# A windowed-attention kernel on one core: the fourth scores of image 0 move to other banks, v's projection and the first bias move ahead of them, and image 1's middle parts are placed behind the first Exp

## The chip, the cores and the metric

The program runs on one core of a Trainium2 chip. The core has five engines with instruction streams of their own: TensorE (PE, matrix products), VectorE (DVE), ScalarE (ACT), GpSimd (POOL) and SyncE (SP, which here only issues transfers), and 16 DMA engines shared by all queues. The engines wait for each other on counting semaphores. The metric is the device time of one execution in microseconds (us); lower is better.

## The reference

One block of a shifted-window transformer on 8 images of 16 x 128 tokens with 32 channels; windows of 4 x 32 tokens (16 windows for each image, N = 128 tokens each), 4 heads of 8 channels:

```python
y = _layernorm(x, g1, b1)
y = jnp.roll(y, (-SH, -SW), axis=(1, 2))
xw = windows(y)                                    # (B * NWIN, N, DIM)
qkv = (xw @ qkv_w + qkv_b)
q, k, v = (qkv[0] * SCALE, qkv[1], qkv[2])
attn = jnp.einsum('bhid,bhjd->bhij', q, k) + bias + mask
attn = jax.nn.softmax(attn, axis=-1)
o = jnp.einsum('bhij,bhjd->bhid', attn, v) @ proj_w + proj_b
x = x + unroll(o)
z = _layernorm(x, g2, b2)
z = gelu(z @ fc1_w + fc1_b) @ fc2_w + fc2_b
return x + z
```

The lines `windows` and `unroll` stand for the reshapes of the reference; `bias` is a relative-position table and `mask` hides windows' foreign regions.

## The kernel before

**Units of work.** The 128 windows are taken in 64 pairs (PAIRS), 8 pairs an image. For a pair j the kernel computes the scores twice: scores 1 (`bias_s1`, `scores_s1`, query rows on the partitions), of which DVE takes the row maximum (`row_max`, L524, into `negm`), and scores 2 (`bias_s2`, `scores_s2`, key rows on the partitions), into which the maximum has already been fed as extra rows of q, and of which ACT takes the exponential (`exponential`, L735, into `prob`). `weighted_values` (L945) multiplies the exponentials with v. For every two pairs (a group k) PE transposes the maxima (`transpose_max`, L863), ACT rounds them to bf16 (`high_max`, L730, `m_hi`), DVE takes what is left (`middle_max`, L530, `m_mid`), and SP sends both into `q_rows` (`send_max`, L262); the first scores 2 of the group wait for these transfers (semaphores d_m0 and d_m1).

**Each image's preparation.** PE transposes the normalized image (`transpose_first`, L839), ACT copies it (`copy_yT`, L708), PE projects q and k (`project_qk`, L845) and v (`project_v`, L851). q and k are then split into three bf16 parts: the high part by ACT (`high_part`, L713), the remainder by DVE (`remainder`, L515), the middle part by ACT (`middle_part`, L719), the low part by POOL (`low_part`, L394), each for two halves. SP stores a part in DRAM (`scatter`, L250) and twelve gathers (`gather`, L212, each 16 x 8 x 512 bf16, 128 KB) bring the parts back as rows. The scores 1 of an image's first pair wait for all twelve (`scores_s1`: semaphore d_qk); for image 1 that is pair 8. Image 0 takes a shorter way for its first pairs and is not gathered whole.

**PSUM.** Two banks each: `ps1`, `ps2`, `pq` (halves Q0 and Q1); one bank each: `pav`, `pch`. Scores 1 of pairs 1 and 3 are put in ps2 by `first_home`, all others in ps1. Scores 2 are always in ps2, and the projection of v of image 0 and the transposes of image 2 both use Q0.

**What sets the order.** No scheduler: every engine has a hand-written loop over p from -4 (LEAD = 4) to 63, and what stands in iteration p runs in the order of the `if` lines. Scores 1 run four pairs ahead: iteration p issues scores 1 of pair p + 4 and scores 2 of pair p. Iterations -4 to -1 are the opening. A bank is free for the next bias only when its reader is done: `bias_s1(j)` waits for j maxima, `bias_s2(j)` for j exponentials.

The lines that matter in the opening are `pe.wait_ge(max_done, LEAD)` before the first `bias_s2` (L906), the wait for `mmid_done` before `project_qk` in iteration 1 (L1071), and ACT's iteration -1 (L810 to L816), whose `middle_part(1, 0)` and `middle_part(1, 1)` stand ahead of everything of iteration 0.

## Time and profile before

| what | us |
|---|---|
| median of 3 runs | 231.94 |
| the runs | 230.03, 231.94, 233.01 |
| the profiled execution | 230.33 |
| its span (first to last instruction) | 228.5 |
| PE busy in the span | 208.5 |
| DVE, ACT, POOL busy | 165.0, 148.6, 128.2 |

The profiled execution took 230.33 us, of which 228.5 us are the span and 1.8 us lie around it. Its times are counted from the span's start. A row of the timeline has the start, the duration, engine, source line, operation, output and inputs, and in brackets the engine's idle time before it and what ended it. Rows of the same kind that overlap are merged (x8), and the two passes of an fp32 matmul count as two. SPq and ACTq are the issuing of transfers by those engines. A row of a stretch has from:to, its length, the busy us of PE, PE's weight loads, DVE, ACT and POOL (instructions in brackets), PE's granted clock (1.00 is full speed), the mean busy share of the 16 DMA engines and what they moved in GB/s.

### The profile page before, as it was taken

The page shows a single profiled execution, that of the slowest core. Times are in us where ns is not written, and L with a number is a line of the kernel's source. Part 1 is how long each engine was busy: PE and PEld are TensorE (multiplying, and loading weights), DVE is VectorE, ACT ScalarE, POOL GpSimd, SP SyncE. Part 2 cuts the span into 40 slices and gives each one's busy share as a digit, 9 for nine tenths or more (in the row PEclk, how much of TensorE's full clock was granted, in tenths as well). Part 3 has the DMA queues.
Part 4 walks back from the last instruction along what each step waited for, and adds up shares of the span by engine and source line. Part 5 has one row for each costly group of instructions (what it writes and reads, how often), then busy time and mean ns, then how long its engine had stood idle before and what let it go on. Part 6 is the DMA issues. An engine that isn't in the chain of part 4 may idle for free.

```text
span 228.5 us, 8108 instructions
## 1 busy us (share of the span) xinstructions
PE 208.5 (91%) x3342; PEld 118.3 (52%) x3342; DVE 165.0 (72%) x253; ACT 148.6 (65%) x217; POOL 128.2 (56%) x116
## 2 busy tenths in 40 slices
PE   0779966899999999999999999999999999979884
PEld 0734523556565556655655566566556555443221
DVE  3896756666877777878787877786766757866874
ACT  7475167656676677677757775867555555577883
POOL 8765669272447956794778397632742092160740
PEclk9997999999999999999999999999999999999999
DMA  6826346654524532452255045405520000000233
GB/s 196 244 74 178 108 131 195 177 170 150 165 72 148 164 102 96 144 163 80 95 166 163 11 136 166 122 10 164 179 83 4 6 6 4 1 3 0 105 127 138
DMA packets 24284, 25.41 MB, mean 111 GB/s; under 512 B 3556, under 2 KB 21732, under 8 KB 24164
## 3 DMA queue, kind: packets, MB, share of 16 engines
q1 hardware_dynamic: 23496, 24.16, 34.0%
q10 hardware_dynamic: 752, 0.74, 1.2%
q8 instruction: 26, 0.43, 0.8%
q14 instruction: 10, 0.08, 0.1%
HBM read 16.24 MB, written 8.39 MB: 108 GB/s over the span
## 4 chain that ended last, share of the span: by engine, by line
issue 39%; POOL 36%; PE 10%; ACT 6%; DVE 3%; DMA 2%; SPq 1%; POOLq 1%; ACTq 0%; DVEq 0%
POOL rstd L376 17%; POOL X L406 4%; POOL parts L394 4%; POOL yn L386 3%; POOL X L411 3%; POOL xc L368 3%; PE ps L962 3%; DMA slots<-parts 2%; ACT q_rows L740 1%; POOL mean L356 1%; ACT k_rows L740 1%; POOL var L362 1%; PE pq L962 1%; PE pav L992 1%; ACT k_rows L745 1%
## 5 line engine op out<-in xcount | busy, mean ns | idle before, releaser
L524 DVE TENSOR_REDUCE negm<-ps 128x8 f32<-128x1024 f32 x64 | 78.2, 1223 | 32.7 <-PE ps L898 32.5
L735 ACT ACTIVATE prob<-ps 128x1024 f32<-128x1024 f32 x64 | 65.5, 1023 | 39.7 <-PE ps L925 39.6
L376 POOL TENSOR_TENSOR rstd<-var,neghalf 128x16 f32<-128x16 f32 x16 | 47.4, 2962 | 17.3 <-DVE var L489 16.4
L912 PE MATMUL ps<-rel_j,id_b 96*32 96x512 bf16 x512 | 39.5, 381 | 3.1 <-ACT prob L735 2.9
L945 PE MATMUL pav<-prob,va 128*32 128x128 f32 x1024 | 41.1, 279 | 0.0
L945 PEld LDWEIGHTS pav<-prob,va 128*32 128x32 f32 x1024 | 24.1, 109 | 12.5 <-issue 5.0
L876 PE MATMUL ps<-rel_i,ident_b 64*64 64x512 bf16 x256 | 26.7, 407 | 0.2 <-DVE negm L524 0.2
L925 PE MATMUL ps<-q_rows,k_rows 64*128 64x128 bf16 x512 | 25.4, 219 | 0.4 <-DMA q_rows<-m_mid 0.4
L898 PE MATMUL ps<-k_rows,q_rows 64*128 64x128 bf16 x512 | 25.2, 219 | 0.0
L394 POOL TENSOR_TENSOR parts<-rest,parts 128x512 bf16<-128x512 f32 x15 | 17.3, 1158 | 13.6 <-ACT parts L719 13.6
L925 PEld LDWEIGHTS ps<-q_rows,k_rows 64*128 64x128 bf16 x512 | 14.4, 94 | 15.5 <-issue 14.6
L730 ACT ACTIVATE m_hi<-pq 16x128 bf16<-16x128 f32 x32 | 8.5, 265 | 16.6 <-PE pq L863 16.5
L356 POOL TENSOR_SCALAR mean<-ssum 128x16 f32<-128x16 f32 x11 | 2.8, 257 | 29.0 <-DVE ssum L471 28.6
L898 PEld LDWEIGHTS ps<-k_rows,q_rows 64*128 64x128 bf16 x512 | 17.0, 95 | 1.3 <-issue 1.3
L876 PEld LDWEIGHTS ps<-rel_i,ident_b 64*64 64x64 bf16 x256 | 7.2, 103 | 18.2 <-DVE negm L524 7.9
L912 PEld LDWEIGHTS ps<-rel_j,id_b 96*32 96x32 bf16 x512 | 11.8, 96 | 9.0 <-ACT prob L735 8.5
L530 DVE TENSOR_TENSOR m_mid<-pq,m_hi 16x128 bf16<-16x128 f32 x32 | 8.6, 270 | 8.7 <-ACT m_hi L730 7.4
L386 POOL TENSOR_TENSOR yn<-xc,rstd 128x512 f32<-128x512 f32 x13 | 13.9, 1071 | 1.0
L368 POOL TENSOR_TENSOR xc<-X,mean 128x512 f32<-128x512 f32 x12 | 12.6, 1048 | 1.7 <-DVE yn L504 0.8
L362 POOL TENSOR_SCALAR var<-vsum 128x16 f32<-128x16 f32 x11 | 2.2, 203 | 19.9 <-DVE vsum L483 19.6
L471 DVE TENSOR_REDUCE ssum<-X 128x16 f32<-128x512 f32 x16 | 10.9, 681 | 2.7 <-DMA X<-x_tok 2.5
L515 DVE SCALAR_TENSOR_TENSOR rest<-pq,qk_bias,parts 128x512 f32<-128x512 f32 x12 | 8.9, 745 | 4.3 <-ACT parts L713 4.3
(134 smaller groups left out, 333.8 us busy)
## 6 DMA issues: line engine op xcount, KB each, us to landing
slots<-parts SPq DMA_DIRECT2D x21, 256.0 KB, 2.4
q_rows<-slots SPq DMA_DIRECT2D x42, 128.0 KB
k_rows<-slots SPq DMA_DIRECT2D x40, 128.0 KB
X<-x_tok SPq DMA_DIRECT2D x8, 256.0 KB, 4.0
y_tok<-res SPq DMA_DIRECT2D x7, 256.0 KB, 2.0
q_rows<-m_hi SPq DMA_DIRECT2D x32, 4.0 KB
q_rows<-m_mid SPq DMA_DIRECT2D x32, 4.0 KB
bias_parts<-rel_parts SPq DMA_DIRECT2D x3, 128.0 KB
```

The lines of the kernel that those rows point to most:

```text
L368: pool.tensor_tensor(per_window(xc[:, i, :]), per_window(img(n)), mean[:, i, :].unsqueeze(2).to_broadcast([128, WPI, C]), ALU.subtract).th ...
L376: pool.tensor_tensor(rstd[:, i, :], var[:, i, :], neghalf[:], ALU.pow).then_inc(rstd_done[i], 1)
L386: pool.tensor_tensor(per_window(yn[:, i, :]), per_window(xc[:, i, :]), rstd[:, i, :].unsqueeze(2).to_broadcast([128, WPI, C]), ALU.mult).t ...
L394: pool.tensor_tensor(parts[:, n % 2, LOW, u, :], rest[:, u, :], parts[:, n % 2, MID, u, :], ALU.subtract).then_inc(lo_done, 1)
L471: dve.tensor_reduce(ssum[:, i, :], per_window(img(n)), AX.X, ALU.add).then_inc(sum_done[i], 1)
L524: dve.tensor_reduce(dst, first_home(j)[:].rearrange("p (a u n) -> p a u n", u=2, n=TOK), AX.X, ALU.max, negate=True).then_inc(max_done, 1)
L735: act.activation(prob[:, j % NPROB, :], ps2[:], ACT.Exp).then_inc(exp_done, 1)
L876: pe.matmul(home[64 * c:64 * (c + 1), 512 * e:512 * (e + 1)], ident_b[64 * e:64 * (e + 1), 64 * e:64 * (e + 1)], rel_i[64 * e:64 * (e + 1) ...
L898: mm = pe.matmul(home[:, 512 * e + at:512 * e + at + TOK], q_rows[64 * e:64 * e + 64, b % NBUF, rows], k_rows[64 * e:64 * e + 64, b % NBUF ...
L912: pe.matmul(ps2[32 * c:32 * (c + 1), 512 * e:512 * (e + 1)], id3_b[0:96, :], rel_j[0:96, c, e].unsqueeze(2).to_broadcast([96, 2, 2, TOK]), ...
L925: mm = pe.matmul(ps2[:, 512 * e + at:512 * e + at + TOK], k_rows[64 * e:64 * e + 64, b % NBUF, rows], q_rows[64 * e:64 * e + 64, b % NBUF, ...
L945: mm = pe.matmul(pav[32 * h:32 * (h + 1), 128 * (j % 4):128 * (j % 4 + 1)], va[:, b % 2, at:at + 32], prob[:, j % NPROB, src:src + 128], s ...
```

## The change

Three edits, all in the opening; every instruction of before is still there.

1. `first_home(3)` is ps1, not ps2. So ps2 is free for `bias_s2(0)` as soon as two maxima are done (the wait for LEAD becomes one for 2), and `bias_s1(3)` must now wait for 3 maxima and not 2.
2. On PE, iteration -1 begins with `project_v(0)` and `bias_s2(0)`, ahead of scores 1 of pair 3. In iteration 0 the transposes of image 2 and `scores_s2(0)` come first, and `transpose_max(1)` and `bias_s1(4)` follow.
3. On ACT, image 1's two middle parts move from iteration -1 to behind the Exp of pair 0. What needs them moves too: on SP the scatter of the middle part goes from iteration -2 to 0, the two low gathers from iteration 0 to 2, behind the maxima of group 2; on ACT the two gathers of the middle part of k go from iteration 0 to 2, behind the Exp of pair 2. On DVE, `middle_max(1)` goes ahead of image 3's sums, and `row_max(5)` ahead of image 2's first remainder.

```diff
--- before.py
+++ after.py
@@ -118,7 +118,7 @@
         FC1 = (ps1, pq, ps2)
 
         def first_home(j):
-            return ps2 if j in (1, 3) else ps1
+            return ps2 if j == 1 else ps1
 
         def mlp_home(m, lo):
             return (pav, pch)[m % 2] if m < B - 1 else (Q1 if lo else Q0)
@@ -287,12 +287,13 @@
                     gather(sp, b + 1, LOW, 1)
                 if p == -2:
                     scatter(1, HIGH)
-                    scatter(1, MID)
                     gather(sp, 1, HIGH, 0)
                 if p == 0:
+                    scatter(1, MID)
+                    gather(sp, 1, HIGH, 1)
                     scatter(1, LOW)
-                    gather(sp, 1, HIGH, 1)
                     gather(sp, 1, MID, 0)
+                if p == 2:
                     gather(sp, 1, LOW, 0)
                     gather(sp, 1, LOW, 1)
                 if p == 3:
@@ -635,11 +636,15 @@
                 n = b + 2
                 if p % 4 == 0 and 0 <= (p - 8) // 4 < OCTETS:
                     add_attention((p - 8) // 4)
+                if p == 0:
+                    middle_max(1)
                 if s == 0 and 3 <= b + 3 < B:
                     dve.wait_ge(d_x[b + 3], 16)
                     sums(first_norm(b + 3), b + 3)
                 if p % 4 == 2 and 0 <= (p - 6) // 4 < OCTETS:
                     normalize((p - 6) // 4)
+                if p == 1:
+                    row_max(p + LEAD)
                 if p >= 0 and n < B and s in (1, 3):
                     remainder(n, s // 2, (Q1, Q0)[s // 2])
                 if s == 6 and 0 <= b - 2 < B - 2:
@@ -653,9 +658,9 @@
                     square_sums(second_norm(b - 1))
                 if s == 7 and b == B - 1:
                     scale(second_norm(b - 1))
-                if p % 2 == 0 and 0 <= (p + 2) // 2 < GROUPS:
+                if p and p % 2 == 0 and (p + 2) // 2 < GROUPS:
                     middle_max((p + 2) // 2)
-                if 0 <= p < PAIRS - LEAD:
+                if 0 <= p < PAIRS - LEAD and p != 1:
                     row_max(p + LEAD)
                 if s == 4 and b == B - 1:
                     dve.wait_ge(x2_done, 2 * b)
@@ -804,6 +809,9 @@
                 if 0 <= p < PAIRS:
                     exponential(p)
                 if p == 0:
+                    middle_part(1, 0)
+                    middle_part(1, 1)
+                if p == 2:
                     gather(act, 1, MID, 1)
                 if p >= 0 and n < B and s in (1, 3):
                     middle_part(n, s // 2)
@@ -812,8 +820,6 @@
                     values(0)
                     high_part(1, 0, pav[:])
                     high_part(1, 1, pch[:])
-                    middle_part(1, 0)
-                    middle_part(1, 1)
                 if s == 3 and 3 <= b + 3 < B:
                     square(first_norm(b + 3))
                 if s == 5 and 0 <= b - 1 < B - 2:
@@ -867,8 +873,8 @@
                 if j < 2:
                     pe.wait_ge(q_first, 1)
                     pe.wait_ge(k_first, 1)
-                elif j < LEAD:
-                    after(pe, max_done, j - 1)
+                elif j == 2:
+                    pe.wait_ge(max_done, 1)
                 else:
                     pe.wait_ge(max_done, j)
                 for c in range(2):
@@ -903,7 +909,7 @@
 
             def bias_s2(j):
                 if j == 0:
-                    pe.wait_ge(max_done, LEAD)
+                    pe.wait_ge(max_done, 2)
                     pe.wait_ge(d_relj, 16)
                     pe.wait_ge(ident_ready, 2)
                 after(pe, exp_done, j)
@@ -1077,17 +1083,22 @@
                         pe.wait_ge(rest_done, 2 * n + 2)
                     project_v(b + 1)
 
+                if p == -1:
+                    project_v(0)
+                    bias_s2(0)
                 if p < 0:
                     bias_s1(p + LEAD)
                     scores_s1(p + LEAD)
                 if p == -3:
                     pe.wait_ge(q_first, 2)
                     keep_busy(3, Q0[:, 0:128])
-                if p == -1:
-                    project_v(0)
+                if p == 0:
+                    pe.wait_ge(va_done, n - 1)
+                    transpose_first(n, Q0)
+                    scores_s2(p)
                 if 0 <= p - AV_LAG < PAIRS:
                     weighted_values(p - AV_LAG)
-                if 0 <= p < PAIRS:
+                if 0 < p < PAIRS:
                     bias_s2(p)
                 if p % 2 == 0 and 0 <= (p + 2) // 2 < GROUPS:
                     transpose_max((p + 2) // 2)
@@ -1097,11 +1108,7 @@
                     project_qk(1, (pch[:], pav[:]))
                 if 0 <= p < PAIRS - LEAD:
                     bias_s1(p + LEAD)
-                if p == 0:
-                    pe.wait_ge(va_done, n - 1)
-                    transpose_first(n, Q0)
-
-                if 0 <= p < PAIRS:
+                if 0 < p < PAIRS:
                     scores_s2(p)
                 if 0 <= p < PAIRS - LEAD:
                     scores_s1(p + LEAD)
```

On PE, from the first group's transposed maxima (L863) to image 2's projection (the last row of each); `ps1<-rel_i` is a bias of scores 1, `ps1<-k_rows,q_rows` scores 1, `ps2<-rel_j` a bias of scores 2, `ps2<-q_rows,k_rows` scores 2, and `pq<-wv_s,yT` v's projection. Before:

```order
L845 MATMUL pav<-yT,wqk_s 128x512
L876 MATMUL ps2<-rel_i,ident_b 64x512 [waits max_done]
L898 MATMUL ps2<-k_rows,q_rows 128x128 x8
L851 MATMUL pq<-wv_s,yT 128x128 x4
L912 MATMUL ps2<-rel_j,id3_b 32x512 [waits ident_ready,d_relj,max_done]
L863 MATMUL pq<-par,negm 16x128 [waits yT_done,mmid_done,max_done]
L876 MATMUL ps1<-rel_i,ident_b 64x512 [waits max_done]
L839 MATMUL pq<-par,yn 128x128 [waits yn_done0,va_done]
L925 MATMUL ps2<-q_rows,k_rows 128x128 [waits d_m0]
L898 MATMUL ps1<-k_rows,q_rows 128x128 [waits d_aux0,d_first]
L845 MATMUL pq<-yT,wqk_s 128x512 [waits yT_done,mmid_done]
```

and after the change:

```order
L851 MATMUL pav<-yT,wqk_s 128x512
L857 MATMUL pq<-wv_s,yT 128x128 x4
L918 MATMUL ps2<-rel_j,id3_b 32x512 [waits ident_ready,d_relj,max_done]
L882 MATMUL ps1<-rel_i,ident_b 64x512 [waits max_done]
L904 MATMUL ps1<-k_rows,q_rows 128x128 x8
L845 MATMUL pq<-par,yn 128x128 [waits yn_done0,va_done]
L931 MATMUL ps2<-q_rows,k_rows 128x128 [waits d_m0]
L869 MATMUL pq<-par,negm 16x128 [waits yT_done,mmid_done,max_done]
L882 MATMUL ps1<-rel_i,ident_b 64x512 [waits max_done]
L904 MATMUL ps1<-k_rows,q_rows 128x128 [waits d_aux0,d_first]
L851 MATMUL pq<-yT,wqk_s 128x512 [waits yT_done,mmid_done]
```

The scores 1 of pair 3 (now in ps1) stand behind v's projection and the first bias of scores 2; the second transposed maxima and the bias for pair 4 stand behind the scores 2 of pair 0.

On ACT, from behind image 1's high parts on, with the Exps (`prob<-ps2`), the parts of images 1 and 2 and the k_rows gathers. Before:

```order
L719 ACTIVATE parts<-rest 128x512 [waits rest_done] x2
L708 ACTIVATE yT<-pq 128x512 [waits vp_done,yTp_done0]
L730 ACTIVATE m_hi<-pq 16x128 [waits mT_done]
L735 ACTIVATE prob<-ps2 128x1024 [waits s2_done]
L212 DMA k_rows<-slots 16x8x512 [waits zero_k1,d_scr_mid]
L212 DMA k_rows<-slots 16x8x512
L713 ACTIVATE parts<-pq,qk_bias 128x512 [waits d_scr_hi,qk_done]
L735 ACTIVATE prob<-ps2 128x1024 [waits s2_done]
L719 ACTIVATE parts<-rest 128x512 [waits d_scr_mid,rest_done]
L713 ACTIVATE parts<-pq,qk_bias 128x512 [waits d_scr_hi,qk_done]
L730 ACTIVATE m_hi<-pq 16x128 [waits d_m0,mT_done]
L735 ACTIVATE prob<-ps2 128x1024 [waits s2_done] x2
```

and after the change:

```order
L713 ACTIVATE yT<-pq 128x512 [waits vp_done,yTp_done0]
L735 ACTIVATE m_hi<-pq 16x128 [waits mT_done]
L740 ACTIVATE prob<-ps2 128x1024 [waits s2_done]
L724 ACTIVATE parts<-rest 128x512 [waits rest_done] x2
L718 ACTIVATE parts<-pq,qk_bias 128x512 [waits d_scr_hi,qk_done]
L740 ACTIVATE prob<-ps2 128x1024 [waits s2_done]
L724 ACTIVATE parts<-rest 128x512 [waits d_scr_mid,rest_done]
L718 ACTIVATE parts<-pq,qk_bias 128x512 [waits d_scr_hi,qk_done]
L735 ACTIVATE m_hi<-pq 16x128 [waits d_m0,mT_done]
L740 ACTIVATE prob<-ps2 128x1024 [waits s2_done]
L212 DMA k_rows<-slots 16x8x512 [waits zero_k1,d_scr_mid]
L212 DMA k_rows<-slots 16x8x512
```

The two middle parts (x2, `parts<-rest`) moved behind the first Exp, and the two gathers from behind the first Exp to behind the third.

On SP, from group 1's m_mid to image 1's last low gather; `slots<-parts` are scatters, `q_rows<-m_hi` and `q_rows<-m_mid` the maxima. A piece of the difference:

```order
 L262 DMA q_rows<-m_mid 2x8x128 [waits mmid_done]
-L250 DMA slots<-parts 128x2x512 [waits lo_done]
+L250 DMA slots<-parts 128x2x512 [waits mid_done]
 L212 DMA k_rows<-slots 16x8x512 [waits zero_k1,d_scr_hi]
 L212 DMA k_rows<-slots 16x8x512 x2
+L250 DMA slots<-parts 128x2x512 [waits lo_done]
 L212 DMA q_rows<-slots 16x8x512 [waits zero_q1,d_scr_mid]
 L212 DMA q_rows<-slots 16x8x512
+L262 DMA q_rows<-m_hi 2x8x128 [waits mhi_done]
+L262 DMA q_rows<-m_mid 2x8x128 [waits mmid_done]
 L212 DMA q_rows<-slots 16x8x512 [waits zero_q1,d_scr_lo]
 L212 DMA k_rows<-slots 16x8x512 [waits zero_k1,d_scr_lo]
```

The middle scatter, and behind it the low scatter, come later, and the maxima of group 2 go out before the two low gathers.

## Rows read from the trace of the kernel before

**Rows 1.** The page's first rows: the span, and each engine's busy time.

```profile
span 228.5 us, 8108 instructions
...
PE 208.5 (91%) x3342; PEld 118.3 (52%) x3342; DVE 165.0 (72%) x253; ACT 148.6 (65%) x217; POOL 128.2 (56%) x116
```

**Rows 2.** Stretches from:to, length, each engine's busy us, granted clock, DMA share, GB/s.

```profile
28.00:32.00 4.00, 2.27 (x33) 1.15 (x33) 2.16 (x4) 3.66 (x8) 2.19 (x3) 1.00 0.20 67
...
36.00:44.00 8.00, 6.15 (x118) 2.97 (x119) 5.01 (x7) 5.07 (x10) 5.38 (x7) 1.00 0.57 173
...
44.00:66.00 22.00, 22.00 (x397) 13.29 (x393) 16.13 (x23) 14.82 (x24) 8.14 (x8) 1.00 0.47 144
```

**Rows 3.** Timeline of PE, 25 to 33 us: start, duration, line, operation, [idle before].

```profile
25.90 0.41 PE L876 MATMUL ps<-rel_i,ident_b 64*64 64x512 bf16 x4
...
26.57 1.16 PE L851 MATMUL pq<-wv_s,yT 128*128 128x128 f32 x8
...
27.97 0.61 PE L912 MATMUL ps<-rel_j,id_b 96*32 96x512 bf16 x8 [0.23 <-DVE negm L524]
...
29.06 0.66 PE L839 MATMUL pq<-par,yn 128*128 128x128 f32 x4
...
32.18 1.13 PE L845 MATMUL pq<-yT,wqk_s 64*128 64x512 f32 x4 [1.91 <-DVE m_mid L530]
```

**Rows 4.** Timeline of ACT, 28 to 39 us.

```profile
28.89 0.69 ACT L713 ACTIVATE parts<-pch,qk_bias 128x512 bf16<-128x512 f32 x1
...
29.89 1.29 ACT L719 ACTIVATE parts<-rest 128x512 bf16<-128x512 f32 x2 [0.31 <-DVE rest L515]
...
31.56 0.25 ACT L730 ACTIVATE m_hi<-pq 16x128 bf16<-16x128 f32 x1
...
31.72 1.00 ACT L735 ACTIVATE prob<-ps 128x1024 f32<-128x1024 f32 x1
...
33.36 1.22 ACTq L212 DMA_DIRECT2D k_rows<-slots  x2
...
34.68 0.69 ACT L713 ACTIVATE parts<-pq,qk_bias 128x512 bf16<-128x512 f32 x1 [1.97 <-issue]
...
35.27 1.01 ACT L735 ACTIVATE prob<-ps 128x1024 f32<-128x1024 f32 x1
...
36.25 0.63 ACT L719 ACTIVATE parts<-rest 128x512 bf16<-128x512 f32 x1
...
38.40 1.02 ACT L735 ACTIVATE prob<-ps 128x1024 f32<-128x1024 f32 x1 [0.41 <-PE ps L925]
```

**Rows 5.** Timeline of DVE, 25 to 37 us: maxima, m_mid, remainder.

```profile
25.49 2.42 DVE L524 TENSOR_REDUCE negm<-ps 128x8 f32<-128x1024 f32 x2
...
31.84 0.28 DVE L530 TENSOR_TENSOR m_mid<-pq,m_hi 16x128 bf16<-16x128 f32 x1 [0.74 <-ACT m_hi L730]
...
35.47 0.75 DVE L515 SCALAR_TENSOR_TENSOR rest<-pq,qk_bias,parts 128x512 f32<-128x512 f32 x1 [2.22 <-ACT parts L713]
```

**Rows 6.** Timeline of POOL: image 2 normalized.

```profile
27.74 1.05 POOL L386 TENSOR_TENSOR yn<-xc,rstd 128x512 f32<-128x512 f32 x1
```

**Rows 7.** Timeline of PE: scores 2 of pair 4, scores 1 of pair 8.

```profile
43.45 0.40 PE L925 MATMUL ps<-q_rows,k_rows 64*128 64x128 bf16 x8 [0.41 <-DMA q_rows<-m_mid]
...
43.69 0.39 PE L898 MATMUL ps<-k_rows,q_rows 64*128 64x128 bf16 x8
```

**Rows 8.** SP's queue: three k gathers, the last low gather, group 2's m_mid.

```profile
35.52 2.96 SPq L212 DMA_DIRECT2D k_rows<-slots  x3
...
40.51 0.59 SPq L212 DMA_DIRECT2D k_rows<-slots  x1
...
41.74 0.53 SPq L262 DMA_DIRECT2D q_rows<-m_mid  x1
```

**Rows 9.** Stretch in which SP's gathers run, columns as in rows 2.

```profile
40.00:41.00 1.00, 1.00 (x28) 0.65 (x28) 0.57 (x1) 0.20 (x1) 0.45 (x1) 1.00 0.71 223
```

**Rows 10.** Line L212, 25 to 50 us: issue duration ns min/median/max.

```profile
L212 SPq DMA_DIRECT2D k_rows<-slots x4: 590/598/1681, 35.5 to 40.5; - x4
```

## Prediction

> **What bounds the kernel now.** I read the stretches first. From 44 us on PE is busy for all 22.00 us of the first full image's 22.00 us at granted clock 1.00, and the page gives PE 91% of the span [rows 1, 2]. The chain of waits ends over POOL, but POOL idles there; the PE rows decide. So a microsecond won after 44 us would have to come out of PE's work, and this change adds and removes no instruction. Before 44 us it is different: between 28 and 32 us PE works 2.27 of 4.00 us, between 36 and 44 us 6.15 of 8.00 us [rows 2]. What the change can win is idle time of PE in the opening, and what it wins shows as the start of PE's full stretch moving left. I take as its mark the scores 1 of pair 8, the first pair of image 1, now at 43.69 us [rows 7]; everything behind it slides with it.
>
> The largest hole is the 1.91 us before image 2's projection at 32.18 us [rows 3]. It is ended by DVE's m_mid (31.84 to 32.12 us) [rows 5], which waits for ACT's m_hi at 31.56 us, and ACT came to that late since two middle parts of image 1 (29.89 us, 1.29 us long) and a copy stood ahead of it [rows 4]. The second hole is before Exp 1: ACT issues two gathers at 33.36 us (1.22 us), so its high part starts only at 34.68 us, 1.97 us after the last work, and Exp 1 at 35.27 us [rows 4].
>
> **The change, walked through.** All times are worked out from the rows; small starts of 0.05 to 0.1 us are included.
>
> PE. Bias and scores 1 of pair 3 took 25.90 to 26.57 us, 0.67 us. With them behind, v's projection starts at 25.90 us and not 26.57 us, and ends at about 27.0 us; ACT's high parts, which follow it, end at 28.9 us and not at 29.58 us. The first bias of scores 2 (0.61 us) takes PE to 27.6 us; it needs two maxima only, so its old wait of 0.23 us is gone. Scores 1 of pair 3 end at 28.3 us. Their maximum (half of 2.42 us, now done at 27.91 us) runs from 28.3 to 29.5 us: 1.6 us later than now. This is the price of the edit. POOL's normalized image 2 is there at 28.79 us, so the transposes run from 28.85 to 29.5 us, against 29.06 to 29.72 us now, and scores 2 of pair 0 end at 29.9 us. The second transposed maxima follow and need the late maximum (29.5 us): there is 0.4 us to spare, so the price is covered [rows 3 to 6].
>
> ACT and DVE. Without the middle parts ahead, m_hi of group 1 ends at 30.45 us (31.81 now) and Exp 0 starts at 30.35 us (31.72 now). But m_mid does not come as early: on DVE two remainders of 0.75 us stand ahead of it, behind the late maximum, from 29.5 to 31.0 us, so m_mid ends at 31.25 us and the projection starts at 31.3 us, 0.9 us earlier than now [rows 3 to 5].
>
> Pair 1: from 31.3 us the projection (1.13), a bias of scores 2 (0.61), a bias and the scores (0.34 and 0.40) give Exp 1 at 33.85 us with 0.1 us for the fourth maximum, since image 3's sums now stand ahead of it; ACT has by then done Exp 0, the middle parts (to 32.65 us) and the high part. Exp 1 is 1.4 us earlier. Pair 2: the maximum of pair 5 now stands ahead of image 2's remainder, which therefore ends at about 36.0 us, hardly before the 36.22 us of now; ACT's copy of it (36.25 us now) comes at 36.1 us, and high part and m_hi follow. Exp 2 starts at 37.4 us instead of 38.40 us: 1.0 us is left [rows 4, 5]. From there to pair 4 the order is the old one. Scores 2 of pair 4 start at 43.45 us after 0.41 us of waiting for m_mid's transfer; that transfer goes out ahead of the low gathers now, so the wait falls away as well. The mark stands, as far as the engines go, at 43.69 - 1.0 - 0.41 = 42.3 us: **1.4 us is the upper bound of the gain** [rows 4, 7].
>
> SP and the transfers. The mark waits for all twelve gathers of image 1. Now the last is issued at 40.51 us [rows 8]. Between the maxima of group 1 and that gather SP now issues 1 scatter, 3 + 2 gathers and the two low ones; after, it issues also the middle scatter and the two transfers of group 2's maxima: 0.4 + 0.55 + 0.53 = 1.5 us more. Its start is 0.6 us earlier with the high parts. One of the three k gathers took 1.68 us to issue against a median of 0.60 [rows 8, 10]; it followed ACT's two gathers. If the long one is gone, the last gather goes out at 40.51 + 1.5 - 0.6 - 1.1 = 40.3 us; if it returns behind ACT's gathers, which now stand behind Exp 2 at 38.4 to 39.7 us, at 41.4 us. To land it needs no more than the 2.9 us from 40.51 us to 43.45 us, at which the transfer issued behind it had landed [rows 7, 8], and I take 2.4 us. So the rows of image 1 are there between 42.7 and 43.8 us, middle 43.2 us, which is later than 42.3 us. **I expect a gain of 43.7 - 43.2 = 0.5 us**, between 0 and 1.0 us.
>
> POOL gets the middle parts 1.5 us later and its low parts with them, but SP reaches the low scatter only at about 36.5 us, and POOL had idle time before; this costs nothing unless the low scatter were to stand ahead of the k gathers.
>
> A word on bytes: between 40 and 41 us the queues moved 223 GB/s at a share of 0.71 [rows 9]. ACT's two gathers (256 KB) left their place before SP's rush and stand in it now; at that rate they need 1.2 us of the DMA engines beside the last four gathers. The Trainium skill, "DMA: Bandwidth & Descriptors", section "Issuing engines are not separate DMA queues", says that transfers of all issuing engines run on the same 16 DMA engines and interleave, so that a second queue saves only issue time. Taken at its word it adds those 1.2 us to the landing, 44.4 us at the middle, and the kernel is slower by 0.7 us; the trace, with its share of 0.71, leaves room for part of it.
>
> **The sum.** 228.5 - 0.5 = 228.0 us of span, 229.8 us for an execution like the profiled one (230.33). The median of the runs shown, 231.94 us, is 1.6 us above that execution, so I place the median after at 231.94 - 0.5 = 231.4 us.
>
> **The rivals.**
> - *The rows of image 1 come in time*: SP's long issue is gone and the gathers land before 42.3 us. For it: between 36 and 44 us the DMA share is only 0.57 [rows 2]. Against it: the low gathers wait for the low scatter, and seven transfers are issued serially. Gain 1.4 us: 230.5 us. Chance 0.2.
> - *Nothing*: the rows land about as late as the mark of now, and each 0.1 us won is idle time before pair 8. 231.9 us. Chance 0.15.
> - *Slower*: the rows land later than 43.7 us; this is the point from which it decides, and PE has then nothing else to do, as v's projection and the weighted values of pair 3 are queued behind. With the long issue (41.4 us), 2.9 us to land and ACT's bytes (1.2 us) it is 45.5 us, a loss of 1.8 us: 233.7 us; half of that at the middle, 232.8 us. Chance 0.2.
> - *The maxima become the limit*: DVE's remainders ahead of m_mid take longer than thought, and the projection stays near 32.18 us. Then Exp 1 still gains from ACT's free time; 231.7 us. It lies inside the forecast.
>
> **The numbers.** The forecast (gain 0.2 to 1.0 us) has 0.45, and the three rivals 0.2, 0.15 and 0.2. The likeliest gives 231.4 us. The runs of before spread from 230.03 to 233.01 us, more than any case here moves, so the range takes the profiled execution with the larger gain (230.33 - 1.3 = 229.0) to the median with the slower case (233.0). Two per cent is 4.6 us, about what a measurement of this kernel can tell from no change. The holes of the opening that could be won are near that in sum (1.73 us of 28 to 32, 1.85 us of 36 to 44 [rows 2]) and cannot all close: faster 0.02. To be slower by 4.6 us the rows of image 1 would have to land at 48 us: 0.03. Within 2%: 0.95.
>
> **What would show it.** In the changed kernel's timeline: v's projection at 25.9 us; transposed maxima of group 1 about 30 us and m_mid ended at 31.3 us; image 2's projection at 31.3 us with a hole below 1 us; Exp 0, 1 and 2 at 30.4, 33.9 and 37.4 us. No wait for m_mid's transfer before scores 2 of pair 4, and instead a wait for a gather before scores 1 of pair 8, which start at 43.2 us. PE full from there, and the span shorter by the same amount. Wrong would be: a mark later than 43.7 us (the slower rival), a mark at 42.3 us without a wait (the first rival), or a shift at the mark that is not found again at the end.

## The result, and the profile of the changed kernel

The changed kernel is slower. Its executions have a median of 234.3 us (4, from 233.04 to 236.09); beside them the kernel before has 231.31 us (4, from 230.03 to 233.01). The ratio is 1.018, with a 95% interval of 1.011 to 1.025: some 3 us more, on the other side of the forecast and above its range. Four later executions (label a1) gave 1.018 again.

The profiled execution took 233.04 us. First rows of its page (columns of the groups: busy us, mean ns of one, idle just before them and what ended it):

```profile
span 231.2 us, 8108 instructions
...
PE 209.2 (90%) x3342; PEld 118.9 (51%) x3342; DVE 164.9 (71%) x253; ACT 148.6 (64%) x217; POOL 128.3 (55%) x116
...
L904 PE MATMUL ps<-k_rows,q_rows 64*128 64x128 bf16 x512 | 24.8, 216 | 2.5 <-DMA k_rows<-slots 2.5
...
L931 PE MATMUL ps<-q_rows,k_rows 64*128 64x128 bf16 x512 | 25.4, 219 | 0.6 <-DMA q_rows<-m_mid 0.6
```

2.7 us were added to the span [rows 1] and only 0.7 us of it to PE's busy time. The wait before scores 1 (L904) is new: 2.5 us, once, for the gathered rows of k. The stretches, columns as in [rows 2]:

```profile
28.00:32.00 4.00, 3.09 (x33) 1.49 (x37) 3.85 (x6) 2.63 (x6) 0.89 (x2) 1.00 0.24 77
36.00:44.00 8.00, 4.88 (x101) 2.43 (x97) 3.57 (x5) 4.89 (x9) 6.62 (x7) 1.00 0.62 189
44.00:50.00 6.00, 5.17 (x63) 3.84 (x64) 2.00 (x3) 1.60 (x3) 2.68 (x2) 0.72 0.52 173
50.00:66.00 16.00, 16.00 (x292) 9.16 (x290) 11.71 (x17) 10.07 (x17) 5.21 (x6) 1.00 0.46 137
```

From 28 to 32 us PE works 0.8 us more than in [rows 2]. That alone does not show the hole filled by the edit: an execution of the kernel before with its clock at 1.00 in the opening (label b2) has 3.13 us there. From 24 to 32 us together it is 6.73 us after against 5.86 us in b2, and this 0.9 us is the filled idle time. From 36 to 44 us PE works 1.3 us less than in [rows 2]. From 44 to 50 us it falls short of full, and at a mean granted clock of 0.72, so that part of the stretch ran at the lower of the two levels. From 50 us on all is as before. PE's timeline (start, duration, line, operation, [idle before]; L857 is v's projection, L845 the transposes of image 2, L851 its projection, L931 scores 2, L904 scores 1):

```profile
25.20 1.16 PE L857 MATMUL pq<-wv_s,yT 128*128 128x128 f32 x8
...
28.91 0.63 PE L845 MATMUL pq<-par,yn 128*128 128x128 f32 x4 [1.24 <-POOL yn L387]
...
30.75 1.13 PE L851 MATMUL pq<-yT,wqk_s 64*128 64x512 f32 x4
...
41.89 0.40 PE L931 MATMUL ps<-q_rows,k_rows 64*128 64x128 bf16 x8 [0.62 <-DMA q_rows<-m_mid]
44.83 0.40 PE L904 MATMUL ps<-k_rows,q_rows 64*128 64x128 bf16 x8 [2.54 <-DMA k_rows<-slots]
45.16 2.08 PE L857 MATMUL pq<-wv_s,yT 128*128 128x128 f32 x8
...
49.15 0.40 PE L931 MATMUL ps<-q_rows,k_rows 64*128 64x128 bf16 x8
```

The mark, scores 1 of pair 8, stands at 44.83 us instead of 43.69 us [rows 7]. Behind it v's projection takes 2.08 us and not 1.16 us, and scores 2 of the next pair start 4.32 us after the mark, against 2.75 to 2.77 us where the clock stays at 1.00 (experiments e1 and e4): 1.6 us for the clock. 1.1 + 1.6 = 2.7 us, the whole difference between the two profiled executions. Against b2 it is 1.4 + 1.6 = 3.0 us, and the spans differ by 2.9 us. ACT's and DVE's timelines (L740 is Exp, L724 the middle parts; on DVE L531 is m_mid):

```profile
30.29 1.00 ACT L740 ACTIVATE prob<-ps 128x1024 f32<-128x1024 f32 x1
31.19 1.13 ACT L724 ACTIVATE parts<-rest 128x512 bf16<-128x512 f32 x2
...
33.25 1.02 ACT L740 ACTIVATE prob<-ps 128x1024 f32<-128x1024 f32 x1 [0.36 <-PE ps L931]
...
36.66 1.00 ACT L740 ACTIVATE prob<-ps 128x1024 f32<-128x1024 f32 x1
```

```profile
30.41 0.28 DVE L531 TENSOR_TENSOR m_mid<-pq,m_hi 16x128 bf16<-16x128 f32 x1 [0.15 <-ACT m_hi L735]
```

Exp 0, 1 and 2 are earlier than in [rows 4] by 1.4, 2.0 and 1.7 us, m_mid than in [rows 5] by 1.4 us. Part of that is this execution's clock (below); in any case the engines came earlier, and the end of the opening did not. SP's queue says why:

```profile
33.92 2.95 SPq L212 DMA_DIRECT2D k_rows<-slots  x3
36.92 0.59 SPq L250 DMA_DIRECT2D slots<-parts  x1
...
39.51 0.52 SPq L262 DMA_DIRECT2D q_rows<-m_mid  x1
41.22 0.56 SPq L212 DMA_DIRECT2D q_rows<-slots  x1
41.88 0.56 SPq L212 DMA_DIRECT2D k_rows<-slots  x1
```

SP sends the low scatter (L250) at 36.92 us, finishes with m_mid's transfer of group 2 at 40.03 us, and has then nothing to do but the two low gathers. It issues them at 41.22 and 41.88 us, since they wait for that scatter to land: 4.3 us after its issue. The last of them is in 2.95 us after its issue. In [rows 8] the last gather had gone out at 40.51 us, *ahead* of m_mid. The DMA engines in the 40 slices of 0.25 us from 36 to 46 us (first line tenths busy, second GB/s):

```profile
DMA  0367384789799999897400001047447954854976
GB/s 16 70 209 234 111 270 152 201 266 258 258 361 356 357 352 299 258 316 255 130 29 25 20 0 33 0 131 242 152 115 221 340 209 164 262 197 115 287 238 254
```

Between 38 and 40.5 us they move up to 361 GB/s; from 41.0 to 42.5 us almost nothing, while PE waits. From 41.0 us on the wait is not for bandwidth but for an order: landing of the scatter, issue, landing. Whether the scatter itself landed late because of the traffic over it (mean DMA share 0.80 from 36.9 to 41.2 us), these rows don't separate.

### The profile page after: what moved, and what is told of

The parts are those of the page before. It is cut to its first block, busy times and chain, and to the rows that moved or that the text cites. A ratio compares the mean times of both kernels' runs of the same rounds, so it can differ in the third digit from the quotient of the medians.

```text
span 231.2 us, 8108 instructions
## 1 busy us (share of the span) xinstructions
PE 209.2 (90%) x3342; PEld 118.9 (51%) x3342; DVE 164.9 (71%) x253; ACT 148.6 (64%) x217; POOL 128.3 (55%) x116
## 4 chain that ended last, share of the span: by engine, by line
issue 43%; POOL 41%; PE 6%; ACT 4%; DVE 3%; DMA 2%; POOLq 1%; DVEq 0%
POOL rstd L377 18%; POOL parts L395 5%; POOL X L407 4%; POOL yn L387 4%; POOL xc L369 3%; POOL X L412 3%; PE ps L968 2%; DMA X<-x_tok 2%; ACT q_rows L745 1%; POOL mean L357 1%; POOL var L363 1%; ACT k_rows L745 1%; PE pq L968 1%; PE pav L998 1%; POOL va L335 1%
## 5 line engine op out<-in xcount | busy, mean ns | idle before, releaser
L740 ACT ACTIVATE prob<-ps 128x1024 f32<-128x1024 f32 x64 | 65.5, 1024 | 40.0 <-PE ps L931 39.9
L951 PE MATMUL pav<-prob,va 128*32 128x128 f32 x1024 | 41.6, 281 | 0.0
L951 PEld LDWEIGHTS pav<-prob,va 128*32 128x32 f32 x1024 | 24.3, 110 | 12.7 <-issue 5.3
L904 PE MATMUL ps<-k_rows,q_rows 64*128 64x128 bf16 x512 | 24.8, 216 | 2.5 <-DMA k_rows<-slots 2.5
L882 PE MATMUL ps<-rel_i,ident_b 64*64 64x512 bf16 x256 | 26.2, 400 | 0.3 <-DVE negm L525 0.2
L931 PE MATMUL ps<-q_rows,k_rows 64*128 64x128 bf16 x512 | 25.4, 219 | 0.6 <-DMA q_rows<-m_mid 0.6
L931 PEld LDWEIGHTS ps<-q_rows,k_rows 64*128 64x128 bf16 x512 | 14.4, 94 | 15.7 <-issue 14.6
L904 PEld LDWEIGHTS ps<-k_rows,q_rows 64*128 64x128 bf16 x512 | 16.7, 94 | 3.8 <-issue 3.8
L531 DVE TENSOR_TENSOR m_mid<-pq,m_hi 16x128 bf16<-16x128 f32 x32 | 8.6, 270 | 9.1 <-ACT m_hi L735 7.8
L1049 PE MATMUL pch<-par,oT 128*128 128x128 f32 x64 | 10.5, 287 | 1.2 <-DVE oT L627 1.2
```

What stands on the lines that cost most here:

```text
L740: act.activation(prob[:, j % NPROB, :], ps2[:], ACT.Exp).then_inc(exp_done, 1)
L882: pe.matmul(home[64 * c:64 * (c + 1), 512 * e:512 * (e + 1)], ident_b[64 * e:64 * (e + 1), 64 * e:64 * (e + 1)], rel_i[64 * e:64 * (e + 1) ...
L904: mm = pe.matmul(home[:, 512 * e + at:512 * e + at + TOK], q_rows[64 * e:64 * e + 64, b % NBUF, rows], k_rows[64 * e:64 * e + 64, b % NBUF ...
L931: mm = pe.matmul(ps2[:, 512 * e + at:512 * e + at + TOK], k_rows[64 * e:64 * e + 64, b % NBUF, rows], q_rows[64 * e:64 * e + 64, b % NBUF, ...
L951: mm = pe.matmul(pav[32 * h:32 * (h + 1), 128 * (j % 4):128 * (j % 4 + 1)], va[:, b % 2, at:at + 32], prob[:, j % NPROB, src:src + 128], s ...
```

## A table to compare like with like

Executions of one kernel differ in when the granted clock is at 0.5, and the opening shifts with it: with 20 to 24 us at 1.00, 0.57 or 0.50, scores 1 of pair 2 stand at 23.3 to 23.6, 24.3 to 24.5 or 25.0 to 26.7 us. I therefore compare the mark only within a class. The last class is the roughest: e2 starts from 25.0 us and b1 from 26.1 us, so that e2's figure is rather too small, and b1 and e10 had a second fall ahead of the mark (0.60 from 36 to 40 us, 0.57 from 40 to 44 us) that e6, for one, did not have. "Before" has an execution in each (labels b2, the profiled one, b1).

| 20–24 us at | kernel: mark, us | against before |
|---|---|---|
| 1.00 | before 43.44; after 44.83 and 44.57; e1 43.73; e4 44.26; e5 43.84; e7b 42.30 | after +1.4, +1.1; e1 +0.3; e4 +0.8; e5 +0.4; e7b −1.1 |
| 0.57 | before 43.69; e3 44.30; e7 43.06 | e3 +0.6; e7 −0.6 |
| 0.50 | before 45.08; e2 46.44; e6 45.11; e8 47.56; e8b 47.05; e10 46.41; e11 48.00 | e2 +1.4; e6 0.0; e8 +2.5; e8b +2.0; e10 +1.3; e11 +2.9 |

The mark carries through to the end. Span less mark is 184.8 to 184.9 us in the ten profiled executions whose clock stays at 1.00 behind the mark (before, b1, b2, e1, e4 to e7b, e10), and 186.3 to 186.5 us in the five where it falls there for a few us (after, a1, e2, e3, e8b); in e8 and e11, where it falls for longer, 187.6 and 187.1 us. So a fall behind the mark costs 1.5 to 1.6 us, and all else that these kernels differ in is decided at the mark.

By the same token one execution is a thin base. Spans of all executions with a mean granted clock of 0.998 or more:

| kernel | span, us |
|---|---|
| before | 227.0 to 229.2, median 227.4 (30); b2 is one of 228.3 |
| e1 | 228.6, 228.8 |
| e2 | 228.8 |
| e3 | 228.5, 228.6 |
| e4 | 229.1 to 230.6, median 230.1 (5) |
| e5 | 228.4 to 228.7 (4) |
| e6 | 227.0 to 227.7 (3) |
| e7 and e7b | 226.2 to 227.1 (8) |
| e8 | 227.4 |
| after and a1, e8b, e10, e11 | none |

b2's mark of 43.44 us is thus late for a "before" at full clock: 227.4 less 184.85 us puts a typical one at about 42.5 us (an estimate), and the losses in the first row of the table are rather too small, by up to 0.9 us.

Against b2, the execution of before at 1.00, the engines' gain has the places that the prediction had, at a third to three quarters of the size: image 2's projection 31.18 → 30.75 us, Exp 1 34.26 → 33.25 us, Exp 2 37.39 → 36.66 us, scores 2 of pair 4 43.21 → 41.89 us. And b2 says one thing more:

```profile
31.18 1.13 PE L845 MATMUL pq<-yT,wqk_s 64*128 64x512 f32 x4 [0.64 <-DVE m_mid L530]
...
43.21 0.40 PE L925 MATMUL ps<-q_rows,k_rows 64*128 64x128 bf16 x8 [1.17 <-DMA q_rows<-m_mid]
43.44 0.39 PE L898 MATMUL ps<-k_rows,q_rows 64*128 64x128 bf16 x8
```

```profile
34.49 3.65 SPq L212 DMA_DIRECT2D k_rows<-slots  x3
...
40.35 0.55 SPq L212 DMA_DIRECT2D k_rows<-slots  x1
...
41.54 0.53 SPq L262 DMA_DIRECT2D q_rows<-m_mid  x1
```

The projection is 1.0 us earlier than in the profiled execution [rows 3], the mark only 0.25 us [rows 7]. The rest is a wait of 1.17 us for the transfer of m_mid, which SP issued at 41.54 us behind its gathers; three k gathers alone held the queue for 3.65 us. With the clock up, the opening of *before* was already bound by SP's queue, in this execution at least. The 0.41 us of [rows 7] was the tip of that wait, and the profiled execution hid it since its engines came late.

## Experiments

Ratios are against the kernel before in runs side by side; the expectations speak of the mark and of distances from scores 1 of pair 2 to it. Where only a part of an edit is shown, dots stand for the rest.

**e1: the edits on PE alone** (fourth scores in ps1 instead of ps2, v's projection and first bias up), all of the middle parts as before.

```
-            return ps2 if j in (1, 3) else ps1
+            return ps2 if j == 1 else ps1
...
+                if p == -1:
+                    project_v(0)
+                    bias_s2(0)
...
```

> Only edits 1 and 2 (bank of pair 3's scores, v's projection and the first bias moved up); ACT, DVE and SP as before. Theory L (the loss comes from image 1's rows, which edit 3 makes late, and from the clock that falls while PE waits for them): no wait for a gather before the scores 1 of pair 8, which start at 43.0 to 43.7 us; ratio to before 0.99 to 1.002. Theory P (PE's new order costs the time, since the maximum of pair 3 is 1.6 us later): the mark is later than 44 us and the ratio above 1.01.

231.83 us (10), ratio 1.0075 (1.002 to 1.013), between the ranges of the two theories: no wait for a gather, but not without a loss either. The late fourth maximum is not free. DVE, ACT and PE:

```profile
27.65 1.23 DVE L524 TENSOR_REDUCE negm<-ps 128x8 f32<-128x1024 f32 x1 [0.84 <-PE ps L898]
28.79 0.74 DVE L515 SCALAR_TENSOR_TENSOR rest<-pav,qk_bias,parts 128x512 f32<-128x512 f32 x1
```

```profile
29.57 1.29 ACT L719 ACTIVATE parts<-rest 128x512 bf16<-128x512 f32 x2 [1.61 <-DVE rest L515]
```

```profile
43.49 0.40 PE L925 MATMUL ps<-q_rows,k_rows 64*128 64x128 bf16 x8 [0.80 <-DMA q_rows<-m_mid]
43.73 0.39 PE L898 MATMUL ps<-k_rows,q_rows 64*128 64x128 bf16 x8
```

The maximum of pair 3 starts at 27.65 us and both remainders behind it; ACT waits 1.61 us for them and has the middle parts 0.7 us later than before at the same clock (29.57 against 28.89 us). With them go the middle scatter and all that SP sends behind it, and the 0.80 us for m_mid at 43.49 us are what is left of that. (In the changed kernel itself this does not bind: the remainders are done at 30.26 us, and the middle parts start at 31.19 us, behind Exp 0.)

**e2: the middle parts and the new order of the transfers alone.**

```
                 if p == -2:
                     scatter(1, HIGH)
-                    scatter(1, MID)
...
                 if p == 0:
-                    scatter(1, LOW)
+                    scatter(1, MID)
                     gather(sp, 1, HIGH, 1)
+                    scatter(1, LOW)
                     gather(sp, 1, MID, 0)
+                if p == 2:
                     gather(sp, 1, LOW, 0)
...
```

> Only edit 3 (image 1's middle parts behind the first Exp, with the moved scatter and gathers); PE's order and banks as before. Theory L: the low gathers are issued at 41 to 42 us, the scores 1 of pair 8 wait 1 to 3 us for them and start at 44.5 to 45.5 us, the clock falls behind that wait, ratio 1.01 to 1.02. Theory P: no such wait, ratio below 1.005.

234.73 us (4), against 230.26 us of before; there is no ratio. By the table +1.4 us at the mark, and the clock fell behind it. At a mean clock of 0.978 its three executions have spans of 232.9 to 233.7 us, where before has a median of 231.2 us and e1, at 0.977 and 0.978, 230.9 to 231.7 us: there this edit loses some 2 us and e1 hardly anything. With the clock at 1.00 its one execution (228.8 us) is no longer than e1's. So most of the loss is in this edit where the clock falls; its share at full clock is not shown.

```profile
44.88 0.40 PE L931 MATMUL ps<-q_rows,k_rows 64*128 64x128 bf16 x8 [1.85 <-DMA q_rows<-m_mid]
46.44 0.40 PE L904 MATMUL ps<-k_rows,q_rows 64*128 64x128 bf16 x8 [1.17 <-DMA k_rows<-slots]
```

Both waits are for SP's queue: m_mid's transfer 1.85 us, the low gather 1.17 us more. The mark is later than the 44.5 to 45.5 us expected.

**e3: after, with the low scatter ahead of the k gathers.**

```
                     scatter(1, MID)
-                    gather(sp, 1, HIGH, 1)
                     scatter(1, LOW)
+                    gather(sp, 1, HIGH, 1)
                     gather(sp, 1, MID, 0)
```

> The changed kernel, but SP issues the scatter of image 1's low part directly behind that of the middle part, ahead of the three k gathers of the high part and not behind them. Theory L, with the low scatter as the late link: it is issued at about 34.2 us instead of 36.9 us, has landed by 38 us, the low gathers go out at 40.0 to 40.8 us directly behind the maxima of group 2, and the scores 1 of pair 8 start at 42.6 to 43.5 us, a wait below 1.2 us, without a fall of the clock: ratio to before 0.985 to 1.0. Rival theory B (the DMA engines' bytes are the limit, with ACT's two gathers among them): the low gathers land at 44 us or later all the same, ratio 1.005 to 1.02.

232.54 us (10), ratio 1.0078 (1.003 to 1.013).

```profile
34.14 1.99 SPq L250 DMA_DIRECT2D slots<-parts  x2
...
40.67 0.56 SPq L212 DMA_DIRECT2D q_rows<-slots  x1
41.33 0.57 SPq L212 DMA_DIRECT2D k_rows<-slots  x1
```

```profile
42.80 0.40 PE L931 MATMUL ps<-q_rows,k_rows 64*128 64x128 bf16 x8 [1.18 <-DMA q_rows<-m_mid]
44.30 0.61 PE L904 MATMUL ps<-k_rows,q_rows 64*128 64x128 bf16 x8 [1.10 <-DMA k_rows<-slots]
```

The low gathers no longer wait for their scatter (40.67 us is right behind m_mid's transfer), so the 1.2 us that SP stood idle in after are gone and 1 per cent of the 1.8 is back. I had expected that to be all. It wasn't: both scatters now pass before the k gathers, PE waits 1.18 us for m_mid, and the last gather is still issued only at 41.33 us and needs 2.97 us. The clock fell here too (0.57 from 44 to 48 us). A mark of 44.30 us and this ratio are inside what the expectation gave to the rival that the engines' bytes are the limit. Against that rival: the gather needs 2.97 us here, with a mean DMA share of 0.57 from 41 to 42 us, and 2.95 us in after, with 0.03 to 0.08 from 41 to 42.5 us; so the traffic at its issue did not set its time. That traffic delays the scatters isn't excluded.

**e4: after, with nine matmuls of no use in the wait before the mark.**

```
+                if p == 4:
+                    pe.wait_ge(rest_done, 6)
+                    keep_busy(BUSY, Q0[:, 0:128])
```

> The changed kernel with 9 matmuls of 128 x 128 (fp32, of no use to the result) in front of the scores 1 of pair 8, where PE waits 2.5 us. Theory L says the wait stays (the scores 1 of pair 8 start at 44.8 us as in the changed kernel), but the clock is 1.00 between 45 and 49 us and the time behind it is 1.4 to 1.7 us shorter: span about 229.6 us, ratio to the kernel before 1.003 to 1.01. If the clock is a matter of its own that falls anyway, the span stays at 231 us.

232.65 us (10), ratio 1.009 (1.003 to 1.015).

```profile
41.58 2.27 PE L1008 MATMUL pq<-par 128*128 128x128 f32 x18
44.26 0.40 PE L905 MATMUL ps<-k_rows,q_rows 64*128 64x128 bf16 x8 [0.41 <-DMA k_rows<-slots]
44.59 1.16 PE L858 MATMUL pq<-wv_s,yT 128*128 128x128 f32 x8
```

PE works through 2.27 us of the wait, 0.41 us of it are left, the last gather is issued at 41.47 us and in at 44.26 us (after: 41.88 and 44.83 us; a1: 41.80 and 44.57 us), and v's projection behind the mark starts at its full speed (scores 2 of pair 5 at 47.03 us, 2.77 us behind the mark). The profiled span is 229.1 us against 231.2 and 231.0 us; of that, 0.6 and 0.3 us are the earlier mark and the rest, 1.5 to 1.6 us, is the clock. Of 10 executions 5 had a mean granted clock of 0.999 or more; of 8 of after, none was above 0.993. The clock is thus 1.5 to 1.6 us of the loss, by the ratios (1.018 and 1.009) about half, and its fall is a consequence of the wait. The other part stays: at a clock of 0.999 or more e4 has spans of 229.1 to 230.6 us, before a median of 227.4 us. How much of this the nine matmuls cost by themselves where the wait was shorter, no run shows. The page that bears on this is the Trainium skill, "TensorE: Matmul & The Clock Gate", Part 1 on the clock gate: the throttled state is the default, activity of the array releases it. The trace agrees, with 1.00 where the wait was filled and 0.59 to 0.64 from 44 to 48 us where it wasn't.

**e5: before, with only the two low gathers behind the maxima of group 2.**

```
                     gather(sp, 1, MID, 0)
+                if p == 2:
                     gather(sp, 1, LOW, 0)
                     gather(sp, 1, LOW, 1)
```

> The kernel before, only with the two low gathers of image 1 issued behind the maxima of group 2 instead of ahead of them (one of the moves of edit 3 by itself). Theory L (whatever is issued last on SP is what PE waits for): scores 2 of pair 4 no longer wait, scores 1 of pair 8 wait 0.3 to 1 us for a gather and start at 43.9 to 44.5 us; ratio 1.001 to 1.005, since the gathers slip only by the 1.1 us of two issues. If it were this move that costs the time of the change, the ratio would be 1.01 or more.

231.35 us (10), ratio 1.008 (1.001 to 1.015).

```profile
42.10 0.40 PE L926 MATMUL ps<-q_rows,k_rows 64*128 64x128 bf16 x8
43.84 0.40 PE L899 MATMUL ps<-k_rows,q_rows 64*128 64x128 bf16 x8 [1.34 <-DMA k_rows<-slots]
```

Here the wait for m_mid is gone (against 1.17 us in before) and 1.34 us for the gather took its place: whichever is last in the queue is waited for. Even alone, this step costs 0.4 us at the mark against b2; at granted clock 1.00 its spans are 228.4 to 228.7 us, and those of before have a median of 227.4 us, a loss of 1.0 to 1.3 us. The ratio is above the 1.001 to 1.005 expected, the mark just ahead of the 43.9 to 44.5 us.

**e6: after without image 1's two low gathers.** The q and k of image 1 lack their low parts, so less is transferred and less awaited.

```
-                if p == 2:
-                    gather(sp, 1, LOW, 0)
-                    gather(sp, 1, LOW, 1)
...
```

> The changed kernel without the two gathers of image 1's low parts (256 KB and two issues; image 1's q and k then lack their low parts). Everything else, the engines' order too, as in the changed kernel. Theory L: the scores 1 of pair 8 wait only for the middle gathers and start at 42.1 to 42.6 us, the clock stays at 1.00, and the whole kernel is 2.5 to 4 us faster than the changed one: ratio to before 0.99 to 0.998. Rival: something of the engines' new order costs the time; then the ratio stays above 1.01.

230.58 us (10), ratio 1.004 (0.998 to 1.009); the mark level with before.

```profile
44.88 0.40 PE L928 MATMUL ps<-q_rows,k_rows 64*128 64x128 bf16 x8 [1.22 <-DMA q_rows<-m_mid]
```

The counts in the waits for image 1's gathers are lowered to match. The wait at the mark itself is gone, and with it the fall of the clock and 1.4 of the 1.8 per cent. What stays is m_mid, 1.22 us. The spans at full clock, 227.0 to 227.7 us, are those of before (median 227.4 us). So with the two gathers removed altogether the edits still win nothing, and the expectation (a mark of 42.1 to 42.6 us, a ratio of 0.99 to 0.998) is missed: the rest of the queue is late as well.

**e7, e7b: e1, with the remainders of image 1 ahead of the fourth maximum on DVE.**

```
             row_max(2)
-            row_max(3)
             remainder(1, 0, pav[:])
             remainder(1, 1, pch[:])
+            row_max(3)
```

> Edits 1 and 2 only (as the run with PE's part only), and on DVE image 1's two remainders stand ahead of the maximum of pair 3 instead of behind it. Theory M (edits 1 and 2 lose since the late maximum holds the remainders, and they hold the middle parts and so every transfer of image 1): the middle parts start at 28.4 to 28.6 us instead of 29.57 us, the middle scatter goes out about 1 us earlier, the scores 1 of pair 8 start at 42.6 to 43.2 us instead of 43.73 us; ratio to before 0.993 to 1.002, against 1.0075 with PE's part only. If the maximum is the limit by itself, image 2's projection starts later than 31.86 us and nothing is won.

> Edits 1 and 2 with the remainders ahead of the maximum of pair 3, a second time and longer, to see whether it is faster than the kernel before. Spans at full clock were 226.2 to 227.1 us against a median of 227.6 us of before, so the ratio should be 0.994 to 0.999.

e7: 230.33 us (10), 0.998 (0.992 to 1.004). e7b: 228.95 us (12), 0.996 (0.992 to 1.001).

```profile
42.07 0.40 PE L925 MATMUL ps<-q_rows,k_rows 64*128 64x128 bf16 x8
42.30 0.39 PE L898 MATMUL ps<-k_rows,q_rows 64*128 64x128 bf16 x8
```

These rows are e7b's. No wait at either (e7 still waits 0.33 us for m_mid), and the mark 1.1 us (e7: 0.6 us) before that of before. The middle parts start at 28.20 us, not at 28.89 or 29.57 us, and SP's whole queue moves with them. Each interval still holds 1. At a mean granted clock of 0.998 or more the spans are 226.2 to 227.1 us in eight executions; those of before reach from 227.0 to 229.2 us in thirty. It is the best version found: by the medians of these 0.6 us, though no ratio shows it.

**e8, e8b: after, with the middle parts in their old place on ACT,** the transfers in the new order.

```
-                if p == 0:
-                    middle_part(1, 0)
-                    middle_part(1, 1)
...
                     high_part(1, 1, pch[:])
+                    middle_part(1, 0)
+                    middle_part(1, 1)
```

> The changed kernel with ACT's two middle parts of image 1 back in iteration -1, ahead of the copy, m_hi and the first Exp; SP's and ACT's transfers stay in the new order, PE's too. Theory S (it is the new order of SP's queue that makes image 1's rows late: the middle scatter stands behind the maxima of group 1, the low scatter behind three more gathers): the middle scatter is issued at 33 us or later although the middle parts are done by 31 us, PE waits 1.5 us or more for a gather before the scores 1 of pair 8, ratio 1.010 to 1.022. Theory M (it is the middle parts' own lateness): the wait is below 1 us and the ratio at most 1.008, as with PE's part only.

> As the run with the middle parts early and the transfers in the new order, a second time and longer, since four executions gave no ratio. Theory S: scores 1 of pair 8 come 20.8 us or more after the scores 1 of pair 2, behind a wait for a gather, and the ratio is 1.008 to 1.02. Theory M: below 20.5 us and at most 1.008.

e8: 233.07 us (4), no ratio. e8b: 233.89 us (6), 1.014 (1.007 to 1.021).

```profile
36.53 0.40 SPq L250 DMA_DIRECT2D slots<-parts  x1
...
44.09 0.56 SPq L212 DMA_DIRECT2D k_rows<-slots  x1
```

In e8b's profile the parts are done at 33.9 us, but SP sends their scatter at 36.53 us, behind the q gathers and the maxima of group 1, and the last low gather at 44.09 us: 2.0 us late at the mark, behind a wait of 1.21 us for a gather (1.5 us or more was expected of it). The ratio is in the range of the theory that blames the order. The distance of 20.36 us is 0.4 us short of it and inside that of the theory that blames the parts' lateness (below 20.5 us); e8's is 21.08 us. So a mark can be as late with the parts done in time, because their scatter waits its turn. The executions as a whole are less plain: both profiles are of the longest execution of their run, and three of e8's four (spans 227.4 us at 0.998, 231.2 and 231.3 us at 0.976 and 0.977) are level with before at such clocks (227.4 and 231.2 us).

**e11: before, with only the middle scatter behind the maxima of group 1,** and ACT's two gathers of it behind Exp 2.

```
                     scatter(1, HIGH)
-                    scatter(1, MID)
                     gather(sp, 1, HIGH, 0)
                 if p == 0:
+                    scatter(1, MID)
                     scatter(1, LOW)
```

> The kernel before, only with the scatter of image 1's middle part moved behind the three q gathers and the maxima of group 1 on SP (and ACT's two gathers of that part behind the Exp of pair 2, as in the changed kernel); the low scatter follows directly, the low gathers keep their place ahead of the maxima of group 2. Theory S: the middle scatter goes out 2 us later than in before and all behind it 0.5 to 1 us later, so the maxima of group 2 reach PE 1 to 2 us later than in before and the scores 1 of pair 8 come 20.0 to 21.0 us after those of pair 2; ratio 1.004 to 1.015. Theory M: no change (below 19.5 us, ratio below 1.003), since the middle parts themselves are as early as before.

236.81 us (4), against 231.01 us of before, no ratio: the highest median of all. At the same mean clock of 0.993 its span is 231.3 us against 228.3 us of before. Only the middle scatter and ACT's two gathers changed their places.

```profile
36.87 1.99 SPq L250 DMA_DIRECT2D slots<-parts  x2
...
42.88 0.54 SPq L212 DMA_DIRECT2D k_rows<-slots  x1
...
44.06 0.53 SPq L262 DMA_DIRECT2D q_rows<-m_mid  x1
```

```profile
47.59 0.61 PE L925 MATMUL ps<-q_rows,k_rows 64*128 64x128 bf16 x8 [3.72 <-DMA q_rows<-m_mid]
```

The two scatters go out at 36.87 us, together; the transfer of m_mid stands behind all gathers at 44.06 us, PE waits 3.72 us for it, and from 48 to 52 us it runs at 0.50. The order of the queue costs this by itself, more than I had expected: the distance is 21.63 us, not 20.0 to 21.0 us.

**e10: before, with five matmuls of no use in the 1.9 us hole ahead of image 2's projection.** The question was whether that hole makes the clock fall in so many executions of before.

```
+                    if p == 1:
+                        pe.wait_ge(rest_done, 4)
+                        keep_busy(5, pch[:, 0:128])
```

> The kernel before with 5 matmuls of 128 x 128 (fp32, of no use to the result) in the hole of 1.9 us ahead of image 2's projection. If the hole is what lets the clock fall between 34 and 40 us in nearly half of the executions of before (mean clock 0.978 instead of 1.00, 3.5 us longer), far fewer than 4 in 10 executions have a clock of 0.985 or less, and the median is about 1 us lower: ratio 0.992 to 0.998. If the fall comes from ahead of it, the share and the time are as before.

232.66 us (4), 1.010 (1.002 to 1.019), mean clocks 0.977 to 0.985: it didn't help. The spans, 230.0 to 231.3 us, are those of before at such clocks (229.1 to 232.1 us), so that the ratio says that none of the four kept the clock up and not that the matmuls cost time. The expectation is missed, and the hole is not what lets the clock fall; in the profile the fall stands at 40 to 44 us (0.57), in b1 at 36 to 40 us (0.60).

**a1, b1, b2** are after and before once more, for executions at other clocks; their marks are in the table. a1 came out as expected. b1 was to show the opening at 1.00 from 20 to 24 us; its clock was 0.50 there, so it doesn't answer its question. b2 was expected 18.9 to 19.4 us from scores 1 of pair 2 to the mark and has 20.13 us: missed, by the wait of 1.17 us for m_mid.

> The changed kernel, unchanged, to have its time and its clock from more than four executions. Theory L: the mark stands at 44 us or later behind a wait for a gather in the profile, hardly any execution keeps a clock of 0.998 or more, and the ratio to before is 1.012 to 1.022.

> The kernel before, unchanged, profiled once more, to see how its opening moves when the clock is at 1.00 from 20 to 24 us (in the first profile it was 0.57 there). If the opening is bound by PE, the scores 1 of pair 8 come 0.6 us earlier than 43.69 us; if POOL, ACT and the transfers bind it, less.

> The kernel before, unchanged, profiled a third time, for a profile at full clock in the opening. Measured from its scores 1 of pair 2 the scores 1 of pair 8 should come 18.9 to 19.4 us later, as in its two other profiles.

## Why the prediction was wrong, point by point

- **What bounds the opening: wrong.** "What the change can win is idle time of PE", read from one execution. It took the holes at 32.18 and 35.27 us as the limit and the 0.41 us for m_mid as a remainder. At full clock before waits 1.17 us there. A chain scatter, gather, m_mid on SP ran beside the engines' chain, 0.41 us longer in the profiled execution and 1.17 us in the other.
- **PE, ACT and DVE: right in place and order, gains smaller.** v's projection (25.2 us, forecast 25.9), m_mid ended at 30.7 (31.3), projection at 30.75 (31.3), Exp 0 to 2 at 30.3, 33.3, 36.7 (30.4, 33.9, 37.4). The times are met or beaten thanks to the clock of this execution; against b2 the projection gains 0.4 us (forecast 0.9) and the three Exps 0.4, 1.0 and 0.7 us (forecast 1.4, 1.4 and 1.0). Scores 2 of pair 4 came 1.3 us earlier of 1.4 us forecast, b2's wait for m_mid included. Their wait for m_mid "falls away as well", it said; 0.62 us of it stayed.
- **"The price is covered" (the late fourth maximum): wrong, though not what decided.** For the transposed maxima it is covered. The remainders stand behind the same maximum; the prediction followed them to m_mid and not to the middle parts, scatter and gathers. e1 puts the price at 0.75 per cent, e7 gives it back. In the changed kernel the middle parts stand behind Exp 0 anyway.
- **SP and the transfers: right in kind, mis-sized, and this is the step that decided.** The forecast of the last gather's issue was 40.3 us, or 41.4 us with the long issue; it was 41.88 us. The long issue stayed (2.95 us for three k gathers) although ACT's gathers were no longer ahead of it, so they are not its reason. The order of the queue would have had the last two gathers out right behind m_mid, at about 40.7 us for the last (an estimate from its end at 40.03 us). And the term for the scatter is missing in the sum: it was named only under the rivals ("the low gathers wait for the low scatter") and never priced; it cost 1.2 us of idle queue, at 4.3 us from issue to landing. The landing of the last gather was taken as 2.4 us, with 2.9 us as a bound; it was 2.95 us here, and 2.77 to 2.97 us in a1, e2, e3, e5 and e8b. In e8 it was 3.60 us. With 41.88 us and 2.9 us the same sum gives 44.8 us. From the forecast mark of 43.2 us to the measured 44.83 us, 1.0 us is the issue (41.88 us, middle of the forecast 40.85 us) and 0.55 us the landing; the 1.6 us for the clock come behind it. The prediction also held that the low scatter ahead of the k gathers would cost time; POOL was done with the low parts at 34.15 us, and e3, with that order, lost less (1.0078 against 1.018).
- **The rule on bytes.** By the word of the Trainium skill, "DMA: Bandwidth & Descriptors", "Issuing engines are not separate DMA queues", the prediction had got a landing at 44.4 us, nearest of all its numbers to 44.83 us. But the reason isn't the one given: the DMA engines lay nearly idle from 41.0 to 42.5 us, and the gather of 41.88 us still took 2.95 us. That they share the bytes may have made the scatter's landing long (the burst of up to 361 GB/s lies over it); no run here separates this.
- **The clock: absent.** Each price of a wait was counted as the wait itself. 2.5 us at the mark cost 1.6 us more behind it; e4 took that away with the transfers in the same order.
- **The rival "Slower"** had the right mechanism, place and point of decision (43.7 us), and a worst mark of 45.5 us; a mark of 44.83 us was worth 231.94 + 1.14 = 233.1 us to it, since it knew nothing of the clock. Its chance was 0.2, and 0.03 for slower by over 2%; the measured 1.8% lies just inside the 2%, its interval (to 2.5%) does not.

**What is open.** Why three k gathers take 1.85 us to issue in one execution (e7b) and 3.65 us in another (b2): traffic does not explain it, since the DMA share over them is 0.89 in e7b and 0.49 in b2. In e3 and e11 they take 1.87 and 1.86 us, but the two scatters ahead of them 1.99 us together, against 0.4 to 0.6 us for one in most of the others. Why the scatter took 4.3 us to land: it stands beside the heaviest traffic, but nothing here varied that alone. How much slower the changed kernel would be with the clock held at 1.00: e4 comes nearest, with matmuls of its own in the count. And what makes the clock low in the opening, so that 34 of 78 executions of before have a mean of 0.977 or 0.978: e10 excludes one place only.

## What to carry to other kernels

Before pricing an engine's gain, follow the queue that issues the transfers as if it were an engine: list its rows in order, and for each ask what must have *landed* for it to go, not only what must be issued. Reordering so that a write to memory and its read back come last puts issue, landing, issue and landing one behind the other, and here that was 4.3 + 0.7 + 2.95 us on the path; keep the scatter early, and keep the work it depends on (the remainders, e7) ahead of work that nothing waits for yet. And a wait of PE may cost more than its length: here 2.5 us of waiting cost 1.6 us more behind it.

## What the runs showed of the hardware

- Executions of one and the same kernel fall into groups by mean granted clock, and the clock is worth more than the change: before has a median span of 227.4 us at 0.998 to 1.00 (30 executions), 228.3 us at 0.993 (7) and 231.2 us at 0.978 (29). The Trainium skill, "TensorE: Matmul & The Clock Gate", Part 1, says that where the clock rises varies between runs of a kernel; the runs agree, with a clock of 1.00, 0.57 or 0.50 from 20 to 24 us in profiles of one and the same kernel. Here it also fell again later in the opening, and the medians lie 3.8 us apart.
- After a PE wait of 2.5 us the granted clock had means of 0.55, 0.50, 0.50 and 0.74 in the four stretches of 1 us from 45 to 49 us (0.50 is the lower of the two levels, 1.2 GHz); after waits of 1.17 us (b2), 1.22 us (e6) and 1.34 us (e5) it stayed at 1.00, and after 1.18 and 1.10 us close together (e3) it fell. So it did after a single wait of 1.21 us at the mark of e8b (0.88 from 44 to 48 us, 0.69 from 48 to 52 us): the length of the wait alone does not decide it.
- A scatter of 256 KB had a median of 2.4 us from issue to landing over the changed kernel (21 of them). The one issued at 33.43 us took 3.2 us, and the one at 36.92 us, beside a mean DMA share of 0.80, took 4.3 us.
- The last gather of 128 KB was in 2.8 to 3.0 us after its issue (after, a1, e2 to e5, e8b; 3.6 us in e8), in after with the DMA engines nearly idle when it was issued (0.03 to 0.08 from 41 to 42.5 us).
